# A convolution and mixture-of-experts block: another order of the chunk stage, another opening, and stores issued from ACT's queue

## The reference, cut to what matters

```python
x = x + relu(grouped_conv3x3(layernorm(x)) + bias)      # 16 images, 16x16, 128 channels, 8 groups
t = x.reshape(4096, 128)
z = layernorm(t)
logits = z @ router_w.T                                  # 8 experts
top-2 experts of each token, softmax over the two logits
t = t + sum over the two experts of share * (silu(z @ gate[e]) * (z @ up[e])) @ down[e]
```

## Time and profile before

| | us |
|---|---|
| median of 3 runs | 247.56 |
| the profiled execution: its time | 248.08 |
| its span, first to last instruction | 245.9 |
| opening, until the first convolution | 0 to 13.7 |
| chunk stage, until the first z_lo of the units is made | 13.7 to 109.5 |
| expert stage, until the last unit's scatter is issued | 109.5 to 228.3 |
| last gathers, additions and stores | 228.3 to 245.9 |
| PE busy / DVE / ACT / POOL, of the span | 75% / 60% / 45% / 58% |
| one indirect DMA's issue on POOL (mean of 64 and 71), and the gap behind it | 0.98, 0.30 |
| highest transfer rate in a fortieth of the span (the opening) | 393 GB/s |

### The profile page before, as it was taken

How to read it: one execution, slowest core, us unless ns; L and a number is a source line. 1 busy time by engine, 2 the same in 40 slices (tenths; PEclk the granted TensorE clock), 3 DMA queues, 4 the chain that set the end, 5 groups by cost and what they waited for, 6 DMA issues and landing times.

```text
span 245.9 us, 4278 instructions
## 1 busy us (share of the span) xinstructions
PE 185.6 (75%) x1079; PEld 160.4 (65%) x1079; DVE 148.1 (60%) x588; ACT 109.9 (45%) x253; POOL 141.8 (58%) x175
## 2 busy tenths in 40 slices
PE   7479849959493984419589999999999999993000
PEld 6467738848382873317478888888888888872000
DVE  2745677494949275533945555555555555579664
ACT  2266495675692736445224444444444444431000
POOL 8132057275778667773777776666666666667100
PEclk9659985979887798557979999999999999999555
DMA  6998001011111126631231255451116961102663
GB/s 195 373 393 278 3 22 55 19 48 46 54 46 52 43 73 150 140 92 32 89 89 53 77 147 135 129 136 55 50 43 200 288 190 45 52 21 103 190 202 120
DMA packets 30262, 27.82 MB, mean 113 GB/s; under 512 B 4488, under 2 KB 24084, under 8 KB 30240
## 3 DMA queue, kind: packets, MB, share of 16 engines
q1 hardware_dynamic: 25616, 18.92, 26.1%
q0 software_dynamic: 4320, 8.43, 10.5%
q10 hardware_dynamic: 304, 0.20, 0.5%
HBM read 16.43 MB, written 11.57 MB: 114 GB/s over the span
## 4 chain that ended last, share of the span: by engine, by line
PE 50%; DVE 27%; ACT 9%; issue 8%; DMA 4%; SPq 1%; DVEq 0%; ACTq 0%
PE ps_y L448 12%; PE ps_gu L365 7%; PE ps_gu L429 7%; PE ps_gu L428 7%; PE ps_gu L430 6%; PE ps_h L438 6%; DVE xt L902 5%; ACT zr L565 5%; PE ps_z L417 3%; DMA zr<-yb 3%; DVE bn L703 2%; ACT relu L542 2%; DVE which L733 2%; DVE xc L696 2%; DMA xt<-x_rows 1%
## 5 line engine op out<-in xcount | busy, mean ns | idle before, releaser
L997 POOL DMA_INDIRECT zs<-zr,slot x64 | 62.8, 982 | 44.3 <-ACT zr L565 22.7
L1010 POOL DMA_INDIRECT yb<-spare,zt x71 | 69.3, 977 | 31.6 <-ACT spare L598 18.2
L365 PE MATMUL ps_gu<-pad,ckw 128*128 128x256 f32 x192 | 54.1, 440 | 6.7 <-issue 6.2
L365 PEld LDWEIGHTS ps_gu<-pad,ckw 128*128 128x128 f32 x192 | 41.3, 223 | 14.5 <-issue 6.7
L882 DVE TENSOR_TENSOR hh<-ps_gu,sg 128x512 f32<-128x512 f32 (+1 forms) x36 | 24.6, 684 | 39.8 <-ACT sg L590 38.6
L448 PE MATMUL ps_y<-wall,hT 128*128 x284 | 38.6, 280 | 1.2 <-DVE hT L891 1.2
L590 ACT ACTIVATE sg<-ps_gu 128x512 f32<-128x512 f32 (+1 forms) x36 | 21.3, 591 | 35.3 <-PE ps_gu L430 35.3
L448 PEld LDWEIGHTS ps_y<-wall,hT 128*128 128x128 f32 x284 | 35.2, 195 | 1.4 <-issue 1.4
L428 PE MATMUL ps_gu<-wall,z_lo 128*128 x71 | 32.2, 454 | 0.0
L429 PE MATMUL ps_gu<-wall,z_hi 128*128 x71 | 29.0, 409 | 0.0
L430 PE MATMUL ps_gu<-wall,z_hi 128*128 x71 | 28.7, 404 | 0.0
(11 more groups left out here) (138 smaller groups left out, 223.8 us busy)
## 6 DMA issues: line engine op xcount, KB each, us to landing
zt<-zs SPq DMA_DIRECT2D x71, 64.5 KB, 2.1
zr<-yb SPq DMA_DIRECT2D x16, 256.0 KB, 4.3
xt<-x_rows SPq DMA_DIRECT2D x8, 256.0 KB, 6.3
xc<-x_cols SPq DMA_DIRECT2D x8, 256.0 KB, 7.4
spare<-gate_up_w SPq DMA_DIRECT2D x8, 256.0 KB, 6.6
out<-xt SPq DMA_DIRECT2D x8, 256.0 KB, 2.0
yb<-spare,zt POOLq DMA_INDIRECT x71, 2.3
wall<-down_w SPq DMA_DIRECT2D x1, 1024.0 KB, 11.2
```

What stands on the lines that cost most here:

```text
L365: last = nc.tensor.matmul(dst, ckw[:, h * BANDS + k, :], pad[n % 2][:, h * IMG:(h + 1) * IMG, below:below + PAIRS, dx:dx + WW], start=k == ...
L997: nc.gpsimd.indirect_dma_start(zs, bass.IndirectOffsetOnAxis(slot[:, k, n * TT + t:n * TT + t + 1], 0), zr[n][:, t, k, :], None, bounds_ch ...
L1010: nc.gpsimd.indirect_dma_start(yb, bass.IndirectOffsetOnAxis(zt[:, u % RING, s, P:P + 1].bitcast(U32), 0), y[:, u % YB, s, :], None, bound ...
```

## The change

- Opening: the first chunk's first two tiles are normalised on DVE (`normalise_first`), ACT does the other two; PE keeps busy with 24 instead of 12 products, then transposes chunk 0 before it touches the router weights, does 6 instead of 4 more and then both halves of conv 0. The router's centring on DVE moves behind pad_odds(0) and stats_x(1); ACT does pad_evens(0) before deviation_x(1).
- First two chunks: conv(1, 0) runs ahead of rows_and_logits(0) and rank(0); transpose_x(2) and conv(1, 1) follow. slots(0), inverse_t(0), normalise_t(0) come before the loop.
- Loop, now from n = 2: DVE does residual(n-1), stats_x(n+3), top_two(n-1), pad_odds(n+1), inverse_x, stats_t(n-1), a weight tail, slots(n-1), inverse_t(n-1). ACT does conv_relu(n-1, 1), normalise_t(n-2), conv_relu(n, 0), copy_rows(n-1), pad_evens(n+1), deviation_x, a weight head, normalise_x(n+2), deviation_t(n-1). PE keeps its order.
- POOL takes four weight tails, DVE four. The first table's row is made one iteration later.
- End: the eight stores go to ACT's queue behind its last y_rows. SP's gathers follow each other with no store between. add_rows(0) to (3) stand in iterations 32 to 35. GATHER_AFTER is 32.

```diff
-DVE_TAILS = {2: [1, 3], 3: [5, 6], 4: [7]}
-POOL_TAILS = [0, 2, 4]
+HEADS = [0, 2, 4, 1, 3, 5, 6, 7]
+POOL_TAILS = HEADS[:4]
+DVE_TAILS = HEADS[4:]
-GATHER_AFTER = 30
+GATHER_AFTER = 32
...
# SP, the end
-            await_results(EARLY)
-            gather_rows(EARLY)
-            for n in range(EARLY):
-                store_rows(n)
-            for n in range(EARLY + 1, CHUNKS):
+            for n in range(EARLY, CHUNKS):
                 await_results(n)
                 gather_rows(n)
-                store_rows(n - 1)
-            store_rows(CHUNKS - 1)
...
# PE
-            keep_warm(12)
+            keep_warm(24)
+            transpose_x(0)
+            keep_warm(6)
+            pe.wait_ge(ckw_ready, 1)
+            conv(0, 0)
+            conv(0, 1)
             pe.wait_ge(rw_step, 3)
             nc.tensor.transpose(ps_h[:, 0:E], rw_c[:], ident[0:E, 0:E]).then_inc(rwT_ready, 1)
-            transpose_x(0)
-            keep_warm(4)
...
+            transpose_x(1)
+            conv(1, 0)
+            pe.wait_ge(rwc_ready, 1)
+            rows_and_logits(0)
+            pe.wait_ge(upper_ready, 2)
+            rank(0)
+            transpose_x(2)
+            conv(1, 1)
+            for n in range(2, CHUNKS + 1):
...
+                if n == EARLY + 2:
+                    table(0, entry1)
+                rows_and_logits(n - 1)
...
# ACT
+            for n in range(2, CHUNKS + 1):
                 conv_relu(n - 1, 1)
                 if n >= 3:
-                    deviation_t(n - 2)
                     normalise_t(n - 2)
+                if n == 2:
+                    normalise_x(3)
                 if n < CHUNKS:
                     conv_relu(n, 0)
                 copy_rows(n - 1)
                 if n + 1 < CHUNKS:
                     pad_evens(n + 1)
+                if n in (2, 4):
+                    deviation_x(n // 2 + 2)
+                if 2 <= n <= 5:
+                    weight_heads(HEADS[n + 2])
+                if 2 <= n and n + 2 < CHUNKS:
                     normalise_x(n + 2)
+                if n < CHUNKS:
+                    deviation_t(n - 1)
...
+            for n in range(CHUNKS):
+                store_rows(n)
...
# DVE
+            def normalise_first():
+                dve.wait_ge(dev1_step, 4)
+                out4 = xn[0][:].rearrange("p (h b) (k c) -> p h b k c", h=CH, k=2)
+                for t in range(TT // 2):
+                    last = nc.vector.tensor_scalar(out4[:, :, t // 2, t % 2, :],
+                                                   xt[:, t, :].rearrange("p (h c) -> p h c", h=CH),
+                                                   mv1[:, t, 0:1], rstd1[:, t:t + 1], ALU.subtract, ALU.mult)
+                last.then_inc(first_half_ready, 1)
...
+            for n in range(2, CHUNKS + 1):
+                residual(n - 1)
+                if n <= 4:
+                    stats_x(n + 3)
+                if n == EARLY + 2:
+                    table_row(0)
+                top_two(n - 1)
+                if n + 1 < CHUNKS:
+                    pad_odds(n + 1)
                 if n in (2, 4):
                     inverse_x(n // 2 + 2)
+                stats_t(n - 1)
+                if 3 <= n <= 6:
+                    weight_tails(DVE_TAILS[n - 3])
+                if n < CHUNKS:
+                    slots(n - 1)
+                    inverse_t(n - 1)
                 if n == EARLY + 1:
                     first_table()
...
-                if u >= UNITS - 2:
-                    add_rows(u - UNITS + 2)
+                if u >= UNITS - 4 and u - UNITS + 4 < EARLY:
+                    add_rows(u - UNITS + 4)
```

More of the change, by code:

```diff
@@ L471, in _ @@
                     conv(n, 1)
-                    if n >= 1:
-                        rank(n - 1)
-                if n == EARLY + 1:
-                    table(0, entry1)
+                    rank(n - 1)
             at = {}
@@ L514, in deviation_x, with normalise_x @@
                 nc.scalar.activation(sd1[:, i], mv1[:, i, 1], ACT.Sqrt, bias=eps[:, 0:1]).then_inc(sd1_ready, 1)
-            def normalise_x(n):
+            def normalise_x(n, first=0):
                 group = [i for i, (c0, c1) in enumerate(X_GROUPS) if c0 <= n < c1][0]
@@ L521, in normalise_x @@
                 out4 = xn[n % 2][:].rearrange("p (h b) (k c) -> p h b k c", h=CH, k=2)
-                for t in range(TT):
+                for t in range(first, TT):
                     i = n * TT + t
@@ L600, in y_rows, with store_rows @@
                                ).then_inc(y_ready, 1)
+            def store_rows(n):
+                act.wait_ge(rows_ready, n + 1)
+                act.dma_start(out[n * N:(n + 1) * N, :].rearrange("(p t) c -> p t c", p=P),
+                              xt[:, n * TT:(n + 1) * TT, :]).then_inc(out_stored, 16)
             act.dma_start(ck[:], conv_k).then_inc(ck_loaded, 16)
@@ L607, in _ @@
             deviation_x(0)
-            normalise_x(0)
-            deviation_x(1)
+            normalise_x(0, first=TT // 2)
             act.wait_ge(pads_zeroed, 2)
             pad_evens(0)
+            weight_heads(HEADS[0])
+            deviation_x(1)
+            weight_heads(HEADS[1])
             normalise_x(1)
             act.wait_ge(bias_loaded, 16)
-            for e in (0, 2, 4):
-                weight_heads(e)
             conv_relu(0, 0)
+            conv_relu(0, 1)
+            pad_evens(1)
             deviation_x(2)
-            pad_evens(1)
-            for n in range(1, CHUNKS + 1):
+            weight_heads(HEADS[2])
+            conv_relu(1, 0)
+            copy_rows(0)
+            normalise_x(2)
+            weight_heads(HEADS[3])
+            deviation_t(0)
+            pad_evens(2)
+            normalise_t(0)
+            for n in range(2, CHUNKS + 1):
                 conv_relu(n - 1, 1)
-                if n == 1:
-                    normalise_x(2)
-                if n in (2, 4):
-                    deviation_x(n // 2 + 2)
                 if n >= 3:
-                    deviation_t(n - 2)
                     normalise_t(n - 2)
+                if n == 2:
+                    normalise_x(3)
                 if n < CHUNKS:
@@ L907, in _ @@
             inverse_x(0)
+            normalise_first()
             dve.wait_ge(ck_loaded, 16)
@@ L915, in _ @@
             dve.wait_ge(pads_zeroed, 2)
+            pad_odds(0)
+            stats_x(1)
             dve.wait_ge(rw_loaded, 16)
             nc.vector.tensor_reduce(rw_sum[:], rw[:], AX.X, ALU.add).then_inc(rw_step, 1)
+            inverse_x(1)
             dve.wait_ge(rw_step, 1)
@@ L921, in _ @@
             nc.vector.tensor_scalar(rw_c[:], rw[:], rw_mean[:], None, ALU.subtract).then_inc(rw_step, 1)
-            pad_odds(0)
-            stats_x(1)
-            inverse_x(1)
+            stats_x(2)
+            stats_x(3)
+            pad_odds(1)
             dve.wait_ge(rwT_ready, 1)
             nc.vector.tensor_copy(rwc, ps_h[:, 0:E]).then_inc(rwc_ready, 1)
+            residual(0)
             dve.wait_ge(masks_made, 4)
```

56 lines of the change are left out of this document (12 added, 44 removed).

## The result

The changed kernel takes 231.98 us (median of 4 runs, 230.25 to 232.42) where the kernel before takes 247.23 in the same comparison: ratio 0.937, 95% interval 0.931 to 0.943. The forecast was 231.8. The profiled spans are 245.9 and 230.6, also 15.3 apart. Two of the terms behind the forecast were off by more than a microsecond, in opposite directions, so I take it apart.

A forecast was written before the change was run, and what follows sets the result against it. PE was taken to bound the expert stage, a chain of hand-overs between ACT and DVE the chunk stage. Span 245.9 - 11.4 (chunk stage) - 4.4 (end) = 230.1, plus 2.2 less 0.5 to the median: 231.8 us; range 228.5 to 239.

The forecast's parts named there:

- The turns of the chunk stage: Six turns from residual(1) to residual(7), each a closed chain of ACT and DVE, plain turn 9.1 us, together 58.1 us.
- One sign: Chunk stage: between residuals, no wait of DVE for logits above 2 us.
- The fifth turn: Chunk-stage turn after the first table's pause, PE late and a half perhaps slow: 9.1 to 12 us, taken 10.0.
- The opening: Start to residual(1): first convolution at 11.3 at full clock, residual(1) at 30.3, bounds 29 and 35.
- the extra POOL tail: 0: POOL's added weight tail (1.3 us) lies ahead of the first dispatch's data, so it costs 0.
- The expert stage moves as a whole: Expert stage, after z_hi: it shifts with the 11.4 us gained, since second table, its loads and dispatch(7) hang on unit numbers.
- The end: Last units to last store: 240.5 against 245.9, 5.4 us gained, 4.4 left after 1.0 for the stores.
- the stores' 1.0: End: 1.0 us taken off for stores running beside the last scatters and gather(7), bounds 0 and 3.
- 1 (the clock): Chunk-stage halves at half clock: 11 us given back, 243, chance 0.09 (mixed case); slower than before, about 265, chance 0.03.
- 2 (the end gives little): Last scatters and gather(7) wait 3 us for stores, slower units cost one: end gives 1.4, 235; chance 0.27 with 3.
- 3 (small waits in the opening): Clock falls or early warmth is missing: residual(1) at 33 to 35 instead of 30.3, 235.5; chance 0.27 together with 2.
- 4 (better than the sum): The stores at the end cost nothing and the turn after the table is 9.1: 230 us; chance 0.1.

The follow-up runs named there:

- e7: Changed kernel with slots and inverse_t of a chunk back in the next turn on DVE, around the next residual: 237.93 us, ratio 0.964 to the kernel before.
- e2: Changed kernel with the end put back as before (stores, additions, GATHER_AFTER): 235.26 us, ratio 0.957 to the kernel before.
- e6: Changed kernel with rows_and_logits(0) ahead of conv(1, 0) on PE and ACT's list reordered to match: 230.52 us, ratio 0.933 to the kernel before.
- e9: The changed kernel again, unaltered, in another comparison: 230.66 us, ratio 0.942 to the kernel before.
- e4: Changed kernel with POOL writing zeros in place of its weight-tail subtractions: 230.26 us, ratio 0.935 to the kernel before.
- e5: Changed kernel with 14 instead of 24 warming products ahead of transpose_x(0): 230.96 us, ratio 0.936 to the kernel before.
- e10: Changed kernel with add_rows(0) to (3) late again, in iterations 34 to 37: 230.73 us, ratio 0.940 to the kernel before.
- e11: Changed kernel with no warming products (no keep_warm): 232.1 us, ratio 0.947 to the kernel before.
- e12: On top of e3, three of POOL's weight tails each wait for a step of DVE's list: 227.63 us, ratio 0.928 to the kernel before.
- e3: Changed kernel with stores 0 to 3 issued by SP ahead of the last gather, ACT keeping 4 to 7: 230.33 us, ratio 0.934 to the kernel before.
- e1: Kernel before with only the end's part of the change: 242.46 us, ratio 0.986 to the kernel before.
- e8: Changed kernel with pad_odds(n+1) behind stats_t(n-1) again: 231.54 us, ratio 0.940 to the kernel before.

## Why the prediction was right, and where it wasn't

**The turns of the chunk stage: four of six right to 0.1 us.** Between residuals I had 9.0, 9.1, 10.0, 11.5, 10.0 and 8.5; the trace has 9.04, 9.09, 10.08, 11.41, 8.63 and 7.64. The first four are the closed chain of ACT and DVE. e7, which puts a link back into it, gives back 6.5 of the 8.3 us between residual(1) and z_hi. Of the residuals only residual(1) waited (1.13 us, until ACT's relu had ended), so PE wasn't their releaser, as forecast. One sign didn't come out: three of the waits for logits were above 2 us (2.72, 2.08 and 2.73), in turns in which no stats_x is left to lie in them; the turns' sum doesn't depend on it.

**The fifth turn: mis-sized, 8.63 for 10.0.** I had 9.1 for the chain and 0.9 for a PE that is late behind the first table's pause. PE was late: it was at half clock there (0.57 granted from 72 to 76). What I had too large was the chain's part, since ACT had done normalise_t (69.17 to 71.25) during the table's work. The other traces with the same code at that place tell the two apart: with 1.00 granted the turn takes 7.94 to 7.99 us (e2, e6, e9), with 0.80 or 0.81 it takes 8.35 to 8.93 (the changed kernel, e4, e5, e10, e11, e12), with 0.65 it takes 9.69 (e3).

**The sixth turn: a call I missed.** pad_odds isn't called in the turn from residual(6) to residual(7), 0.73 us that I left in; 7.64 for 8.5.

**The opening: mis-sized, residual(1) at 31.66 for 30.3.** keep_warm ended at 10.1 and not at 9.1, within the bounds that I gave, and the first convolution started at 11.70 for 11.3. In the other traces the same 48 records took 7.04 to 8.28 us. POOL's part was in no term: its weight tails, costed at nothing because they lie ahead of POOL's first dispatch, hold short DVE instructions for a microsecond each. Two of the three are on the path: 0.5 us at conv(1, 0), which starts 7.50 behind the first convolution in the changed kernel and 7.00 in e12, and 0.85 in slots(0) (1.08 for 0.23). Together 1.35, as e4 and e12 measure. The step that failed is "the extra POOL tail: 0": I asked who waits for POOL's data and not what POOL's instruction does to DVE while it runs. The term meant only the fourth, extra tail; it is the one that held slots(0), the second held the opening's inverse_x(1). Without them residual(1) would have stood at 30.3, as forecast, but in part by luck: the first convolution was 0.4 late, and the rest of the way to residual(1) 0.4 shorter than my 19.0 us (18.6 in e4 and e12).

**From residual(7) to the mark.** z_hi came 12.3 us earlier than before for 11.4 forecast. The expert stage then lost 0.6 of it in its first units (96.22 to 120.43 is 24.2; before 23.6), where the granted clock was 0.62 over 8 us against 0.71 before (and 0.82 in e12, where this stretch takes 22.6). "The expert stage moves as a whole" holds from unit 5 on. At the mark 11.7 are left.

**The end: right in its sequence, mis-sized in its contention.** The early additions cost 1.66 (96.66 from mark to last scatter, 95.0 before), for 2.1. The transfers cost more than the 1.0 that I took: from the last scatter's start to the end I had 240.5 - 229.2 = 11.3 and the trace has 230.6 - 217.09 = 13.5, so 2.2, inside the bounds 0 and 3: 1.1 at the gather's issue (3.38 behind the scatter for 2.3), 0.9 at its landing, 0.3 behind the last addition. The first two are what e3 takes back (2.45 and 4.2). So the term of the sum that was mis-sized is the stores' 1.0; it measured 2.2. The end gives 3.6 for 4.4. I had weighed the Trainium skill (DMA: Bandwidth & Descriptors, section Issuing engines are not separate DMA queues) against the row on the gather's wait. e1 bears out the row: the end without the gathers' waits behind stores has a tail 4.1 us shorter, more than the 8 x 0.34 us of issue. What counts is that no gather waits behind a store, not which queue has the stores: e3 has four of them in SP's queue again and a still shorter tail. What the Trainium skill says there of shared engines agrees with e3: 1 MB issued from ACT's queue beside the last scatters delays them and the gather. e1 changes the stores' queue and their order together; what another order within SP's queue alone would give isn't shown.

**The sum.** 2.2 us too much at the turns, 1.4 too little at the opening, 0.6 at the first units and 0.8 at the end leave a span 0.6 longer than forecast. The step from span to median was 1.4 us (230.6 to 231.98) and not the 1.7 I took, which hides half of it. That 231.8 stands so near 231.98 is in part luck: the terms were off by up to 2.2 us and cancelled. The recorded range of 228.5 to 239, with a chance of one half for the 2 us around the forecast, says better how well the sum was known.

**The rivals.** 1 (the clock) didn't come: 1.00 granted from 30 to 72 us in the changed kernel, and 0.96 in e8, with one slow half. 2 (the end gives little) was half true: 2.2 of its 3 us of contention were there, but the end gave 3.6 us and not 1.4. 3 (small waits in the opening) had the right place, and 1.4 of its 3 to 5 us, for another reason. 4 (better than the sum) had the turn behind the table at 9.1, and it was 8.6; its other half, stores that cost nothing, was wrong by 2.2.

## What to carry to other kernels

Where two engines wait for each other in turn, write the closed chain of one turn from the durations of the old trace and move whatever isn't a link of it into its waits: that was accurate to 0.1 us for four of the six turns here. When work is placed on GpSimd because "nobody waits for it", look at which two-input VectorE instructions run at that moment; a short instruction that is five to eight times as long as elsewhere and ends together with a GpSimd one is the sign. And stores that can leave early should, since at the end they share the DMA engines with the transfer on which everything waits.

## What the runs showed of the hardware that I had not expected

**A GpSimd subtraction holds a short VectorE instruction until its own end.** A DVE instruction with two inputs in SBUF that starts during one of POOL's subtractions (1.27 us) ends with it: 0.92 to 1.31 us instead of 0.16 to 0.29, in the traces of the changed kernel, e2, e3 and e5 to e11, and nowhere in e4 and e12, where the two don't meet. Instructions with one input, and those with one of two inputs in PSUM, kept their durations beside the same subtractions (in the changed kernel the router's reduction at 12.55, and `place` and `base` at 26.09 and 26.16, 0.16 each). In the kernel before POOL's three tails ran back to back from 16.38, and no short DVE instruction with two inputs lay beside them. The Trainium skill (SBUF — State Buffer, section SBUF: two separate sides) states this lock between a VectorE instruction with two SBUF inputs and a GpSimd one that reads SBUF, the first to start keeping the ports for its whole length; the traces agree where GpSimd starts first, and no run here shows the other direction. In e4 a memset, which reads nothing, ran (four of them, 7.21 to 9.12) beside DVE's two-input ckw product, whose 1.75 us was the same as in the changed kernel.

**The phase of the clock spreads a microsecond or two.** The turn behind the table's pause took 7.9 to 9.7 us in traces with the same instructions there, in the order of the granted clock (1.00 down to 0.65). From z_hi to the mark it is 22.6 to 22.9 us where 0.84 is granted (e3, e4, e8, e12) and 23.8 to 24.2 where 0.79 or 0.80 is (the changed kernel, e2, e5, e6, e7, e9, e11). It moves single terms more than most of the edits above do. Terms under 1 us should be read from distances inside one trace, as here.
